# Two-layer graph network with layer norm, one core: one-hot rows made on GpSimd for the second merge, slope and addition of x read from PSUM, statistics by pairs of blocks

## The reference

```python
x = jax.random.normal(..., (100000, 96))
src = jax.random.randint(..., (50000,), 0, 100000)
dst = (100000 * jax.random.uniform(..., (50000,)) ** 2.0).astype(int32)      # then sorted

def _egnn_conv(x, src, dst, edge_attr, W_msg, W_edge, W_root, b):
    msg = x[src] @ W_msg + edge_attr @ W_edge
    agg = jax.ops.segment_max(msg, dst, num_segments=x.shape[0])
    agg = jnp.where(jnp.isneginf(agg), 0.0, agg)
    return agg + x @ W_root + b

c1 = leaky_relu(_egnn_conv(X, src, dst, edge_attr, W1_msg, W1_edge, W1_root, b1))
c2 = leaky_relu(_egnn_conv(c1, src, dst, edge_attr, W2_msg, W2_edge, W2_root, b2))
out = layernorm(x + c2)            # eps 1e-5, slope of leaky_relu 0.01
```

## Time and profile before

| | us |
|---|---|
| median of 3 runs | 1866.52 |
| lowest, highest | 1862.57, 1878.78 |
| the profiled execution's own time | 1874.13 |
| its span in the trace | 1872.3 |

### The profile page before, as it was taken

The page is one execution under the profiler, slowest core; times in us unless marked ns, Lnnn a source line. Parts: engine busy times, 40 slices in busy tenths (PEclk is TensorE's granted clock), DMA queues, the critical chain, the costliest instruction groups (busy, mean ns, idle before and its releaser), DMA issues.

```text
span 1872.3 us, 37110 instructions
## 1 busy us (share of the span) xinstructions
PE 1525.2 (81%) x11422; PEld 1355.2 (72%) x11422; DVE 1315.3 (70%) x2385; ACT 1080.9 (58%) x2450; POOL 1089.0 (58%) x1454
## 2 busy tenths in 40 slices
PE   3998888888889999896889899988987767676663
PEld 2677777777779888885777777777777666576653
DVE  2677677667766655554667777767636789999998
ACT  2354544444543555563555555555527788888887
POOL 6777777767710000004777777777657788675653
PEclk9999999999999999998999999999989899988887
DMA  7778998889875788895878888888767899999996
GB/s 137 212 206 259 285 268 263 263 254 261 261 248 163 239 264 275 284 290 170 223 224 228 238 223 235 233 226 241 205 222 214 248 288 305 296 297 295 294 300 174
DMA packets 505022, 459.13 MB, mean 245 GB/s; under 512 B 348553, under 2 KB 412340, under 8 KB 504836
## 3 DMA queue, kind: packets, MB, share of 16 engines
q1 hardware_dynamic: 444118, 321.15, 60.0%
q0 software_dynamic: 30976, 57.72, 12.3%
q10 hardware_dynamic: 29742, 77.88, 10.6%
HBM read 283.25 MB, written 173.37 MB: 244 GB/s over the span
## 4 chain that ended last, share of the span: by engine, by line
PE 30%; DVE 24%; DMA 20%; POOL 15%; issue 9%; ACT 1%; SPq 1%; DVEq 0%; POOLq 0%; ACTq 0%
PE ps L584 19%; DMA onehot_bytes<-arena_hold 14%; POOL arena_hold L410 12%; DVE stats L953 5%; DMA arena_hold<-nodes,src_perm 4%; DVE arena_hold L896 4%; DVE arena_hold L951 4%; PE ps L495 4%; DVE arena_hold L948 4%; POOL onehot L443 3%; PE ps L463 2%; PE ps L486 2%; DVE arena_hold L882 2%; PE ps L456 2%; DVE arena_hold L971 1%
## 5 line engine op out<-in xcount | busy, mean ns | idle before, releaser
L584 PE MATMUL ps<-arena_hold,onehot 128*128 x4688 | 614.4, 293 | 174.7 <-POOL onehot L443 142.7
L584 PEld LDWEIGHTS ps<-arena_hold,onehot 128*128 128x128 f32 x4688 | 584.1, 206 | 205.3 <-issue 204.2
L410 POOL DMA_INDIRECT arena_hold<-nodes,src_perm x392 | 370.0, 944 | 459.9 <-SPq L377 340.7
L495 PEld LDWEIGHTS ps<-w_root,onehot 97*128 97x128 f32 x3136 | 402.4, 194 | 100.9 <-issue 99.0
L410 POOL DMA_INDIRECT arena_hold<-in_x_dram,src_all x392 | 375.1, 957 | 143.7 <-issue 115.2
L495 PE MATMUL ps<-w_root,onehot 97*128 97x128 f32 x3136 | 418.9, 277 | 0.0
L443 POOL CAST onehot<-keep 128x256 f32<-128x256 uint8 x588 | 302.3, 562 | 117.4 <-PE ps L584 71.6
L648 ACT COPY arena_hold<-ps 128x384 f32<-128x384 f32 x392 | 187.9, 479 | 277.3 <-PE ps L495 275.0
L698 ACT COPY arena_hold<-ps 128x384 f32<-128x384 f32 x392 | 166.7, 477 | 200.3 <-PE ps L584 200.2
L882 DVE TENSOR_TENSOR_SCAN arena_hold<-keep,arena_hold,ps 96x512 f32<-96x512 bf16 x196 | 247.6, 1263 | 42.1 <-PE ps L463 41.8
L896 DVE TENSOR_TENSOR onehot<-count,rel 128x1024 f32<-128x1024 bf16 x147 | 179.5, 1222 | 126.9 <-PE ps L584 126.0
(11 more groups left out here) (99 smaller groups left out, 1160.9 us busy)
## 6 DMA issues: line engine op xcount, KB each, us to landing
root<-arena_hold ACTq DMA_DIRECT2D x196, 384.0 KB
arena_hold<-root SPq DMA_DIRECT2D x196, 384.0 KB, 4.6
nodes<-arena_hold SPq DMA_DIRECT2D x98, 384.0 KB, 3.0
arena_hold<-nodes SPq DMA_DIRECT2D x98, 384.0 KB
arena_hold<-in_x_dram SPq DMA_DIRECT2D x97, 384.0 KB
arena_hold<-in_x_dram SPq DMA_DIRECT2D x48, 768.0 KB, 8.1
out_dram<-arena_hold SPq DMA_DIRECT2D x48, 768.0 KB, 4.7
onehot_bytes<-arena_hold SPq DMA_DIRECT2D x147, 128.0 KB
```

The lines of the kernel that those rows point to most:

```text
L410: nc.gpsimd.indirect_dma_start(out=gathered[t.ring][0:t.p, i, 0:D], out_offset=None, in_=table_in, in_offset=bass.IndirectOffsetOnAxis(ap= ...
L495: last = nc.tensor.matmul(no_ps[m % 2][:, i * P:(i + 1) * P], nodes_t[m % NODE_RING][0:D + 1, i * P:(i + 1) * P], w_root[0:D + 1, layer * ...
L584: nc.tensor.matmul(ps_bytes[:, bass.ds(place_at, SLOT)].bitcast(F32), onehot[:, k % NS, i, :], rows_from(t)[:, bass.ds(word, SLOT)].bitcas ...
```

## The change

**Bytes gone.** `make_bytes`, `store_bytes`, `load_bytes`, the HBM tensor, the buffers and all waits for them are removed. In the second merge GpSimd compares `count` (bf16, 128 columns) with one column of `rel`, 8 times per batch, and writes f32.

**Slope and addition from PSUM.** ScalarE's evacuation in the second merge writes 0.01·y to SBUF instead of y. VectorE takes the maximum of y (PSUM) and 0.01·y (SBUF) back into PSUM, and adds x from PSUM and SBUF into SBUF, half a superblock at a time. A group may be seeded again only after the addition (`x_added`), where before it was after the evacuation.

**Statistics by pairs.** One `bn_stats` reads two blocks interleaved, so that its even statistics are the one block's and its odd the other's. The four small operations disappear; ScalarE's root takes the variance sum straight from `stats`.

**Order and shares.** ScalarE's second merge is written out by halves, its normalisation is split 7 and 5, the seeds of an odd half come after the next evacuation, and those of an even half after the second part of the normalisation. ScalarE normalises 12 blocks, VectorE 4 (14 and 2 for the last two full superblocks).

```diff
@@ gpsimd
-                pool.wait_ge(bytes_in[k // 2 % 2], DMA * (k // 4 + 1))
                 if k >= NS:
                     pool.wait_ge(stepped[1], BATCH * (k - NS + 1))
-                for i in range(0, BATCH, PIECE):
-                    last = nc.gpsimd.tensor_copy(onehot[:, k % NS, i:i + PIECE, :].rearrange("p t n -> p (t n)"), bytes_back(k, 1)[:, 0, i * P:(i + PIECE) * P])
+                for i in range(min(BATCH, T - k * BATCH)):
+                    at = k * BATCH + i
+                    last = nc.gpsimd.tensor_scalar(onehot[:, k % NS, i, :], count[:], rel[:, at:at + 1], None, ALU.is_equal)
                 last.then_inc(grown, 1)
-                if k % 2 and k + 3 < NBATCH:
-                    load_bytes((k + 3) // 2)
@@ tensor, turn_back
-                if t.layer == 0 and t.g >= BYTES_AT:
-                    pe.wait_ge(bytes_made, byte_batches(t.g).stop)
@@ scalar
                 if n >= RING:
-                    act.wait_ge(evacuated[layer], n - RING + 1)
+                    if layer == 0:
+                        act.wait_ge(evacuated[0], n - RING + 1)
+                    else:
+                        act.wait_ge(x_added, (n - RING) // HG + 1)
...
+                        nc.scalar.activation(to, of, ACT.Copy, scale=SLOPE).then_inc(evacuated[1], 1)
...
+            def merge_out():
+                first_seeds(1)
+                for h in range(2 * NSB):
+                    s = h // 2
+                    if h % ENDS == 0:
+                        ends = load_ends(h)
+                    if h % 2 == 0 and s:
+                        deviation(s - 1)
+                    if h % 2 == 0 and s >= 3:
+                        act.wait_ge(out_stored[s % 3], DMA * (s // 3))
+                    act.wait_ge(stepped[1], ends[h % ENDS])
+                    evacuate(1, h)
+                    if h % 2 == 0:
+                        if s:
+                            reseed(1, h - 1)
+                            normalise(s - 1, 0, ACT_FIRST)
+                    else:
+                        if s:
+                            normalise(s - 1, ACT_FIRST, scalar_blocks(s - 1))
+                        reseed(1, h - 1)
...
@@ vector, slope_and_add and normalise_own in place of finish
+                dve.wait_ge(evacuated[1], (h + 1) * HG)
+                nc.vector.tensor_tensor(done, done, y_all.rearrange("p (b j d) -> p b j d", b=HG, d=D), ALU.max).then_inc(sloped, 1)
...
+                    nc.vector.tensor_tensor(y.rearrange("p (b j d) -> p b j d", b=HG, d=D), done, x_rows.rearrange("p (b j d) -> p b j d", b=HG, d=D),
+                                            ALU.add).then_inc(x_added, 1)
...
+                for j in range(0, blocks, 2):
+                    last = nc.vector.bn_stats(stats[:, h % 2 * HG * C // 2 + j // 2, :], y[:, j * D:(j + 2) * D].rearrange("p (h d) -> p d h", h=2))
```

184 lines of the change are left out of this document (75 added, 109 removed).

## The result

| | before | changed |
|---|---|---|
| median, us | 1868.9 (4 runs) | 2074.72 (4 runs, 2072.44 to 2077.55) |
| ratio, 95% interval | | 1.109, 1.106 to 1.113 |
| profiled execution: time, span | 1874.13, 1872.3 | 2077.55, 2075.7 |
| TensorE's mean granted clock | 0.948 | 0.901 |

A forecast was written before the change was run, and what follows sets the result against it. Gathers held up by byte stores were taken to bound the first edge phase, VectorE the late second merge, ScalarE close behind. −33 − 14 + 10 − 3 = −40 us, so 1827 us against the median; range 1800 to 1890.

The forecast's parts named there:

- Bytes gone: First edge phase: without byte comparisons, stores and waits, gathers' 21.3 us of waits and 11.5 of tail go; −33 us.
- the signs: Marks that would show the forecast: first edge phase's gathers ending near 496 us, a first seed near 515.
- The tail: First edge phase, last gather to the merge's first seed: falls from 29.8 to 18.3 us, 11.5 less.
- GpSimd compares: Second merge: each 128-column comparison on GpSimd takes 0.28 us, so a pair of batches costs 4.9 us.
- The upper end: Highest price taken for a GpSimd comparison: 0.393 us, that of a whole 256-column cast alone; the lower end was 0.245.
- first rival: Second merge: comparison too dear, GpSimd sets the pace; 0.34 us gives 1865, 0.37 gives 1898; 25%.
- Early superblocks: Second merge, first ten superblocks: 42 batches at 2.84 us, 0.4 of it handover, make 120; −14 us, bound −27.
- VectorE and ScalarE late: Second merge, last 38 superblocks: VectorE 8.2 us and ScalarE 8.1 each, period 9.4 against 9.14; +10 us.
- The walk's 8.6: Late second merge: stepping through one superblock's order gives 8.6 us if TensorE's steps are always there.
- what is late next: Late second merge: later seeding holds up the ring of PSUM banks; 0.8 us per superblock taken, giving 9.4.
- End: End of second merge: after the last evacuation only half a superblock is left to VectorE; −3 us.
- Statistics by pairs: VectorE's second-merge statistics: stepping between rows costs nothing, starts 0.27 us apart; 0.39 if dear, about 1840, a 12% rival.

The follow-up runs named there:

- run 8: Changed kernel with the one-hot byte path put back and three byte buffers instead of two in the first edge phase: 1824.12 us, ratio 0.976.
- run 7: Kernel before, bytes kept, with only the statistics by pairs: 1855.94 us; the same with ScalarE normalising 12 of 16 blocks instead of 13: 1853.95 us.
- run 1: Changed kernel with the one-hot byte path of before put back, its new finish kept: 1853.32 us, ratio 0.994.
- run 9: Changed kernel with the byte path back and ScalarE seeding an even half's place before the second part of its normalisation: 1840.47 us, ratio 0.988.
- run 4: Changed kernel whose second-merge batches take turns at eight forms of the GpSimd operation, to price each: 1998.94 us.
- run 3: Changed kernel making only one of the eight comparisons per batch, every wait kept: 1800.38 us.
- run 5: Changed kernel with each comparison replaced by a copy of 128 columns (0.244 us), waits and counts kept: 1829.22 us.

## Why the prediction was wrong

**The reading of the bottleneck** was right in the main. The byte stores did hold up the first edge phase (run 8), and late in the second merge VectorE was the bound (between 1480 and 1800 us its slope, addition, statistics and normalisation have 69% of the chain that ended last). What stood close behind VectorE was not ScalarE, though, but GpSimd's stretched casts with TensorE's steps (run 7).

**Bytes gone: right in kind, too large.** −33 was forecast, −27.1 measured at the first seed of the second merge. The last gather starts at 503.6 us, 16.9 earlier, for the 21.3 of its waits: 5.5 us of them stayed. (The "near 496" and "near 515" of the signs are 2 to 3 us below the prediction's own sum, 499 and 517.) The tail fell by 12.4, to 17.4 us, a little more than the 11.5 forecast, so the first seed of the first merge came at 521.0, 29.3 earlier. Then the first merge took 3.1 us longer, 314.9 for 311.8, which the prediction had at nothing; the seven profiles with bytes have 310.6 to 312.7 there and the six without 313.6 to 315.8. No run shows why. The second edge phase gave 0.9 back. One execution can't be read to better than some 3 us: in the five profiles with the same first stages (before and runs 1, 7 and 9) the second edge phase begins anywhere from 857.7 to 863.8 us.

**GpSimd compares: the step that failed.** "I take 0.28, nearest AFFINE_SELECT": it is 0.583 by start to start. Both neighbours misled. IOTA's slope, laid on the cast, gave 0.83 ns per column, which holds for the cast (run 4), and the comparison has 2.5; AFFINE_SELECT compares too, but its 0.28 didn't carry over. The upper end, "the whole cast of 256 columns alone, 0.393", was set by a row that shares only the engine and the kind of operands, and the true price is one and a half times that. No row of the kernel before showed a `tensor_scalar` with a column on GpSimd, and nothing bounded a dearer operation than the cast. The first rival had the right mechanism, and its break-even of 0.34 us lies where the runs put it (0.244 gives 1829, 0.496 gives 1989, 0.583 gives 2075: 1866 lies between 0.30, on the line through the first two, and 0.37, on the line through the last two); but it got 25%, and no price above 0.37. The range was as narrow as its term.

With 0.583 in the forecast's pair of batches, and GpSimd working without a hole as its first rival has it, the pair costs 16 × 0.583 + 0.4 = 9.7 us: 21 pairs make 204 for the early superblocks (202.9 measured), and the remaining 834 steps over 39 superblocks make 13.0 us each (13.5 measured). With −33 and −3 that is about +180 us, for +203 measured. So the mechanism of the loss was on record as a rival; the price that decides between the two was the wrong number.

**Early superblocks.** With the copy of 0.244 us they gain 19.2, for 14 forecast at 0.28 and 27 at 0.245. The 0.4 us of handover per batch was too little.

**VectorE and ScalarE late.** Slope and addition at 0.96 us: 964 and 958 ns. No comparison is stretched: the longest has 738 ns against a median of 611, and a cast's maximum was 2126 before. The walk's 8.6 is 8.82 in run 3. The term "what is late next", 0.8 us for the ring, is confirmed in kind by run 9. (Its 10.3 steps per late half are 834/78 = 10.7 on average, which changes the 0.29 to 0.27.) Its sum of 9.4, or 9.2 with the copy's price, is 9.28 in run 5.

**End.** −3 was forecast; it is −3.8 in the changed kernel and −3.9 with copies, from the slope that ends superblock 47. From the last slope of all to the end it is 10.6 us for 14.0 before. This term was right, and it is the same whether GpSimd is slow or not.

**Statistics by pairs.** Four instructions of 192 columns follow each other at 0.27 us, as priced:

```profile
1804.31 1.16 DVE L937 BATCH_NORM_STATS2 stats<-arena_hold 128x6 f32<-128x192 f32 x4
```

The reading that steps between two rows at every element costs nothing here. The Trainium skill's "Vector Engine (DVE) Microarchitecture Reference" (5.2 Measured stream behaviour on trn2) has 1.73 ns per column for a source that hops at every element, and full rate for a one-source operation that alternates between two regions, there 16 KiB apart; this case, with two rows 96 words apart, agrees with the exception: (1.16 − 0.35)/3 = 0.27 us for 192 columns, 0.35 being the last one's own length, for at least 0.33 by the other figure.

**Left open.** Why the new slope and addition make a late superblock 0.48 us longer than the statistics alone: run 9 explains 0.3 by the order of seeds, the rest isn't shown. Between 1480 and 1800 us GpSimd waited 104.8 us for seeds in run 1 and 1.4 with the statistics alone, and the chain that ended last in run 1 has 29% in the loads of x and 13% in the stores of the result; no run here changes either. That VectorE make part of the comparisons in the changed kernel, where it idles, wasn't tried.

## What to carry to other kernels

Price an operation that no row shows by its own form, or call its price unknown: the same engine, types and columns may hide a factor of three, so the upper end of the range must be looked for among dearer operations, or left far away. Multiply such a price by its count before the range is set: here 0.1 us of error can be 117 us of time. And before a resource is removed because its users wait, try one buffer more: here that gave the same start of the second edge phase (835.8 us for 835.9) and kept the one-hots cheap. And when a change splits a piece of work in halves, compare marks at the same point of the work: the first half's slope in place of the second's would move up to 8 us from one stage to the next.
